# A two-layer decoder on one core: wide rope operations, two norms and a scaling moved, the constants in two transfers, two turns ahead of a bound

## The reference, cut to what matters

```python
x = x + L0_attn(layernorm(x))            # 32 heads, 8 kv heads, rope, a window mask, sinks
x = x + L0_xattn(layernorm(x), mask, ctx)
x = x + L0_ffn(layernorm(x))             # 8 experts, two for each token
x = x + L1_attn(layernorm(x))            # 16 heads of 128, 4 kv heads, rope, causal
x = x + L1_xattn(layernorm(x), ctx, m)   # "readout": softmax(x ctx^T / sqrt(512)) ctx
x = x + L1_ffn(layernorm(x))             # sigmoid * (cos + sin of tanh), 2 rounds of product and norm
# L1_attn:
q = q * cos + rotate_half(q) * sin       # k in the same way
scores = q k^T / sqrt(128);  causal mask;  softmax;  out = attn v;  out @ Wo.T
```

## Time and profile before

| | |
|---|---|
| time, median of 3 | 1766.33 us (1766.12 to 1766.53) |
| the profiled execution | 1767.63 us, its span 1765.8 us |
| busy: PE, DVE, ACT, POOL | 1705.7 (97%), 991.3 (56%), 548.0 (31%), 458.6 (26%) us |
| TensorE's granted clock, mean | 0.991 of full speed |
| the chain that ended last | PE 84%, DVE 9%, POOL 3% |

### The profile page before, as it was taken

How to read it: one execution, slowest core, us unless ns; L and a number is a source line. 1 busy time by engine, 2 the same in 40 slices (tenths; PEclk the granted TensorE clock), 3 DMA queues, 4 the chain that set the end, 5 groups by cost and what they waited for, 6 DMA issues and landing times.

```text
span 1765.8 us, 32976 instructions
## 1 busy us (share of the span) xinstructions
PE 1705.7 (97%) x13868; PEld 1141.1 (65%) x13868; DVE 991.3 (56%) x1965; ACT 548.0 (31%) x1515; POOL 458.6 (26%) x549
## 2 busy tenths in 40 slices
PE   7999999999999999999999999998999999999998
PEld 6776666657666666666546888866677774444444
DVE  3765556537767777677742111125554555664987
ACT  0343334424444444444401111101422222333411
POOL 2532322512322222222022000015131210002676
PEclk9999999999999999999989999999999999999999
DMA  9100012000000000000338988855000033752101
GB/s 400 45 1 1 1 45 70 1 27 20 19 1 19 20 1 19 19 2 1 120 140 333 344 335 330 337 196 192 1 1 1 1 137 118 245 193 84 29 13 42
DMA packets 31844, 172.48 MB, mean 98 GB/s; under 512 B 4008, under 2 KB 4008, under 8 KB 17904
## 3 DMA queue, kind: packets, MB, share of 16 engines
q1 hardware_dynamic: 29456, 163.02, 24.7%
q0 software_dynamic: 2240, 7.34, 1.2%
HBM read 155.67 MB, written 16.52 MB: 98 GB/s over the span
## 4 chain that ended last, share of the span: by engine, by line
PE 84%; DVE 9%; POOL 3%; issue 1%; ACT 1%; DMA 1%; another core or an unknown queue 0%; DVEq 0%; POOLq 0%; SPq 0%; ACTq 0%
PE PS L1308 9%; PE PS L1076 7%; PE PS L1127 6%; PE PS L1486 5%; PE PS L1377 5%; PE PS L1165 5%; PE PS L1317 4%; PE PS L1422 4%; PE PS L1455 3%; PE PS L1188 3%; PE PS L1205 3%; PE PS L1473 3%; PE PS L1135 3%; PE PS L1152 2%; PE PS L1157 2%; DVE R L1606 2%
## 5 line engine op out<-in xcount | busy, mean ns | idle before, releaser
L1308 PEld LDWEIGHTS PS<-R,W 128*128 128x128 f32 x1344 | 153.2, 192 | 11.7 <-issue 11.7
L1308 PE MATMUL PS<-R,W 128*128 128x128 f32 x1344 | 153.6, 275 | 2.2 <-DVE R L1799 2.2
L1622 DVE TENSOR_REDUCE nmw<-PS 112x2 f32<-112x750 f32 x128 | 114.1, 934 | 42.5 <-PE PS L1188 42.5
L2239 POOL TENSOR_TENSOR rstd<-veps,mhalf 128x1 f32<-128x1 f32 (+1 forms) x71 | 53.9, 759 | 322.1 <-DVE veps L1516 298.7
L1076 PE MATMUL PS<-xT,W 128*128 128x224 f32 x640 | 127.2, 358 | 1.0 <-ACT xT L2029 0.7
L1076 PEld LDWEIGHTS PS<-xT,W 128*128 128x128 f32 x640 | 121.8, 193 | 9.8 <-issue 7.6
L1806 DVE TENSOR_TENSOR R<-R,PS 128x512 f32<-128x512 f32 x21 | 14.4, 686 | 199.1 <-PE PS L1308 199.1
L1455 PE MATMUL PS<-W 128*128 128x512 f32 x256 | 119.3, 609 | 0.9 <-ACT R L2097 0.9
L2097 ACT ACTIVATE R<-PS 125x672 f32<-125x672 f32 x128 | 86.6, 730 | 86.2 <-PE PS L1205 86.2
L2265 POOL TENSOR_TENSOR R<-R 128x224 f32<-128x224 f32 x80 | 52.8, 660 | 218.6 <-DVE R L1538 218.5
L1377 PE MATMUL PS<-xT,W 128*128 128x224 f32 x512 | 103.2, 362 | 2.5 <-DVE R L1541 2.3
(11 more groups left out here) (309 smaller groups left out, 3343.5 us busy)
## 6 DMA issues: line engine op xcount, KB each, us to landing
W<-in_we SPq DMA_DIRECT2D x63, 1024.0 KB, 7.6
R<-in_ctxT SPq DMA_DIRECT2D x12, 750.0 KB, 7.1
W<-in_entwT SPq DMA_DIRECT2D x8, 1024.0 KB, 7.0
W<-in_entpw SPq DMA_DIRECT2D x8, 1024.0 KB, 8.6
R<-in_ctx SPq DMA_DIRECT2D x8, 750.0 KB
xs_rows<-in_x SPq DMA_DIRECT2D x3, 1792.0 KB, 36.1
R<-xs_rows SPq DMA_DIRECT2D x21, 256.0 KB, 8.2
ys_rows<-R SPq DMA_DIRECT2D x21, 256.0 KB, 8.2
```

The lines of the kernel that those rows point to most:

```text
L1308: o = e.matmul(PS[:, m, c * 128:(c + 1) * 128], gate_up(j % 3, k, off + c * 128), BT[:, j % 2, k, :], start=k == 0, stop=k == 3)
L1622: e.tensor_reduce(nmw[0:S, par, :].rearrange("p (r f) -> p r f", r=4)[:, r:r + 2, 16 - 16 * par], PS[0:S, r:r + 2, 0:SC], AX.X, ALU.max, n ...
```

## The change

1. **Rope.** For `kq1` (32 steps) DVE does two `tensor_tensor` operations of 448 columns instead of four of 224: one on A and B by the tables cos, sin, one by sin, cos. A second copy of the cosine table, `l1cos_`, stands behind `l1sin` for it. `ku` keeps its four.
2. **Norms of tiles 4 and 5, stage 3**: ahead of round `attend1(1)` instead of ahead of the mask of round 2.
3. **Last unit (u = 3)**: the norm of tile 0 for the readout goes behind the softmax piece `c1` of the first round, that of tile 1 behind the one of the second round, `turn` of tile 0 into the fourth. In all four rounds `d1` stands ahead of the second `v1`, so ahead of its copy on DVE.
4. **Constants**: the first transfer has the columns up to `k0sin` (576 of 2107). The rest goes ahead of `w0o`. The table `spread`, which nothing reads, is gone.
5. **Last stage**: `turnh` 0 and `turnh` 1 stand ahead of the last `bound`.

```diff
@@ constants()
+    CST["later"] = (sum(q.shape[1] for q in parts), 0)
...
     add("l1sin", np.sin(ang))
+    add("l1cos_", np.cos(ang))
...
-    add("spread", spread)
@@ build_order()
-            nxt = norms(3, bs) + nxt[:5] + turns(3, bs) + nxt[5:]
+            nxt = norms(3, bs) * (u > 0) + nxt[:5] + turns(3, bs) + nxt[5:]
...
-            nxt = norms(4, (0, 1)) + turns(4, (0,)) + [("load", "xb", 0)]
+            for n, more in enumerate((norms(4, (0,)), norms(4, (1,)), [], turns(4, (0,)) + [("load", "xb", 0)])):
+                step = attend1(4 * u + n)
+                k = step.index(("c1", u, n, 1)) + 1
+                step.insert(step.index(("v1", u, n - 1, 1) if n else ("v1", u - 1, 3, 1)), step.pop())
+                out += step[:k] + more + step[k:]
+            break
...
-            out += once[4:10] + second + once[10:]
+            out += norms(3, (4, 5)) + once[4:10] + second + once[10:]
...
-    out += [("wave", 3)] + [("bound", t) for t in range(4, NT)]
+    out += [("wave", 3)] + [("bound", t) for t in range(4, NT - 1)]
...
-    out.append(("turnh", 0, *steps[0]))
+    out += [("turnh", n, *steps[n]) for n in range(2)] + [("bound", NT - 1)]
...
-        if n + 1 < len(steps):
+        if 1 < n + 1 < len(steps):
@@ rope_in()
+                if k == "kq1":
+                    both = PS[:, m, 0:2 * UT].rearrange("p (a b n) -> p a b n", a=2, b=UB)
+                    for n, name in enumerate(("l1cos", "l1sin")):
+                        f = CST[name][0]
+                        e.tensor_tensor(T4[:, 2 * n:2 * n + 2, :].rearrange("p a (b n) -> p a b n", b=UB), both,
+                                        cst[:, f:f + 2 * S].rearrange("p (a n) -> p a n", a=2).unsqueeze(2).to_broadcast(
+                                            [128, 2, UB, S]), ALU.mult).then_inc(*up(("rope_half", "rope_in")[n], (k, u, c)))
+                    return
@@ load()
-                    put("d_cst", 0, (cst[:, :], a["consts"]), (col[:, :], a["cols"]))
+                    n = CST["later"][0]
+                    put("d_cst", 0, (cst[:, 0:n], a["consts"][:, 0:n]), (col[:, :], a["cols"]))
...
-                    put("d_w0o", 0, (W[:, 6:10, :], a["w0o"]))
+                    n = CST["later"][0]
+                    put("d_w0o", 0, (cst[:, n:NCST], a["consts"][:, n:NCST]), (W[:, 6:10, :], a["w0o"]))
```

More of the change, by code:

```diff
@@ L133, in constants @@
     add("l1sin", np.sin(ang))
+    add("l1cos_", np.cos(ang))
     add("parity", p[:, None] // 16 % 2 == np.arange(2)[None, :])
-    spread = np.zeros((128, 512), f)
-    spread[:64] = np.arange(512)[None, :] // 16 == np.arange(64)[:, None] % 32
-    add("spread", spread)
     k = np.arange(S)
```

## The result

The changed kernel takes 1756.12 us (median of 5 runs; the kernel before took 1766.33 beside it). The ratio is 0.9939, with a 95% interval of 0.9925 to 0.9953. One of its five runs took 4410.87 us and is not in the ratio. The forecast was 1757.0, the range 1754.0 to 1760.6; by the interval the gain is 8.3 to 13.2 us, so the 0.9 us between forecast and measurement can't be told from none. The profiled execution has a span of 1754.5 us (before 1765.8).

What follows compares the result with a forecast made beforehand. PE, busy in 97% of the span, was taken as the bound, with its waits and the lower clock behind them. The terms summed to 9.35 us; against the median of 1766.33 that gave 1757.0 us, range 1754.0 to 1760.6.

Steps and rivals of the forecast that it cites:

- First transfer: At the start: a shorter first transfer of constants lets the first transposes begin earlier, 0.15 us (bounds 0 and 0.5).
- Wide rope: Projection of unit 0: four ropes ahead of PE's last wait, each 0.13 us shorter, 0.5 us; hidden in units 1 to 3.
- The clock in the projection: Unit 0's projection: a quarter of a chance that the lower clock lasts 3.4 us, not 6.8, saving 1.7; term 0.4 us.
- Norms of tiles 4 and 5: Near 1260: PE's 2.48 us wait and 1.7 of clock go, less 0.4 for `ku`'s copy; 3.8 us.
- First round: Unit 3, first round: with the readout's norms behind the softmax piece, PE's wait of 1.54 us goes; term 1.5 us.
- fourth round: Unit 3, fourth round: earlier `d1` gains 1.0 us, leaves a 0.9 wait, and 1.7 of clock goes; 2.7 us.
- The last stage: Turns ahead of the last bound: copy gives 1.0, with the clock 2.7, but `waved` 6 leaves 0.3 us.
- The clock rivals: New waits, as in unit 3's fourth round or last stage, still drop the clock: 1758.7 or 1760.4 us; chance 0.22.

Runs made afterwards that it cites:

- experiment 3: Only the wide rope for `kq1`, with the table in place of the unused one, on the kernel before; ratio 0.9986.
- Experiment 8: The changed kernel with the last wave (6) one step earlier, ahead of DVE's and POOL's part of product 1; 1754.63 us, ratio 0.9933.
- experiment 1: Only the norms of tiles 4 and 5 moved ahead of round 1, on the kernel before; ratio 0.998.
- experiment 4: Only the two turns put ahead of the last bound, on the kernel before; ratio 0.9989.
- experiment 2: Only the edit of unit 3 (two norms behind softmax pieces, scaling ahead of the copy of the values), on the kernel before; ratio 0.9985.
- experiment 10: The changed kernel with the experts' rows of tiles 4, 5 and 6 added later on DVE; 1755.77 us, ratio 0.9943.
- experiment 11: The changed kernel run once more, nothing altered; 1756.94 us, ratio to the kernel before 0.9942.
- experiment 5: The kernel before with 16 products of 512 columns that nobody reads, in front of five steps where PE waits; 1764.12 us, ratio 0.9993.
- experiment 6: The kernel before with fewer such unread products in the five waits (1, 2, 2, 2, 2); 1764.09 us, ratio 0.999.
- experiment 7: The changed kernel with six unread products of 512 columns at PE's very start; 1754.49 us, ratio 0.9933.

## Why the prediction was right, and where it wasn't

- **First transfer.** Its 0.21 for 0.15 is not shown to be the edit's. In the seven traces with one transfer PE's first transposes start at 7.18 to 7.58 us (mean 7.41), in the four with two transfers at 7.26 to 7.42 (mean 7.33), so the spread is larger than the term. What came behind it, -0.65, is mostly the clock's rise, 1.06 us later in this execution than in that of before (15.85 for 14.79). In the eleven traces without fillers at the start the rise came at 13.1 to 16.0 us, for kernels with the same start too, and PE's lead at 31.5 us follows it, at some 0.5 us for each us.
- **Wide rope.** The price was right: a pair takes 1.14 us from its start to its end, as forecast. It was worth 0.41 (experiment 3), forecast 0.5. By the rule of the Trainium skill (VectorE: DVE Perf Modes, "The DRAIN you can't avoid"), taken without its exception, the term would have been 1.2; the trace disagrees, as the next operation starts 0.53 us behind one that lasts 0.61. The same section adds that an operation that is not held starts earlier, and with that the trace agrees. The step that failed is the one ahead of it, that the waits in the trace of before are the kernel's: 1.03 us of them came from a stall of DVE, probably of that execution alone (experiment 3).
- **The clock in the projection.** "A quarter of a chance of 1.7", 0.4, was mis-sized: it gave 1.26. The 6.8 us were the exception. In eight other traces with a wait of 2.2 to 2.3 us there, the stretch was 3.4 us seven times and missing once.
- **Norms of tiles 4 and 5.** Right: 3.90 for 3.8, with a new wait of 0.36 for `ku`'s copy (0.4).
- **Unit 3.** First round 1.68 for 1.5; fourth round 2.59 for 2.7, with a wait of 0.99 left (0.9). But 1.7 of the fourth round's term is a fall that this wait doesn't always cause.
- **The last stage.** Right: the copy gives 1.04 (forecast 1.0), and `waved` 6 takes back what the clock and the copy give, but for 0.51 (0.3). Experiment 8 shows the cause of the wait that is left.
- **The clock rivals.** The reading of the earlier trace rows, that 1.54 us keep the clock and 1.86 lose it, was too simple. Behind 1.86 us at 1475 the clock fell in 2 of 4 traces (before and experiment 1, not 3 and 4), behind 1.94 at 1650 in 2 of 4 (before and experiment 1 again, not 2 and 3), behind 2.48 at 1260 in 4 of 4. Waits of 1.10 to 1.25 us, which every trace has near 1310, were followed by a fall in 3 of 14, one of 1.5 us near 1447 in none of 6. By the eight cases with 1.9 us (five traces) such a wait costs itself and some 0.85, an estimate. The prediction also passed over layer 0, where much shorter waits were followed by a fall. Windows of the kernel before:

```profile
885.20:892.00 6.80, 5.94 (x49) 2.81 (x44) 0.28 (x1) 1.35 (x2) 0.00 (x0) 0.50 0.02 4
909.10:912.50 3.40, 3.40 (x6) 1.48 (x6) 2.74 (x13) 0.00 (x0) 0.00 (x0) 0.50 0.99 419
```

  Ahead of the first stand waits of 0.73 and 0.82 us, ahead of the second one of 0.78. All 14 traces fall near 886 and 13 near 909, and in the two traces of the table they are equally long, so they left the sum alone, but they speak against any limit near 1.8 us. When the clock rose at the start seems to matter: in the four traces with a rise at 13.1 to 13.4 us (experiments 1, 8, 10, 11) it fell near 747, behind a wait of 0.96, each time; in the seven with a rise at 14.8 to 16.0 never; of the three with fillers at the start (5.0, 5.8, 6.3) in the first two. The Trainium skill (TensorE: Matmul & The Clock Gate, Part 1) says that the clock's watch runs free of the kernel, so that one kernel starts up differently from run to run; the start agrees (13.08 and 15.85 us for the same kernel). That it holds for falls in the middle too would fit these counts, but no run tests it.

So the total came out near the forecast partly since errors of both signs met: 1.65 us too little in the projection, 0.65 too much at the start. The medians are 10.2 us less in the result and 9.5 in experiment 11, not 11.2. There a part of the falls is missing on the side of before: its 69 timed executions have a median granted clock of 0.993 where the profiled one has 0.991. The nine executions of the changed kernel that the two ratios rest on have 0.995, so by an estimate (0.002 of 1764 us) some 3.5 us of the gain are the clock's. That the stall is missing as well is argued, not measured.

What stays open: the cause of DVE's stall, and what decides whether a given wait is followed by the lower clock in one execution and not in the next.

## What to carry to other kernels

Price a wait of the engine that sets the end from the trace, but price the clock behind it from several executions: here one profile held a stall of 1.0 us, and falls that other traces with the same waits lacked (two of them behind waits of 1.9 us). Before a wait is removed, read what the same stage waits for next (wave 6), and ask whether that one only stands in the wrong place of a queue; moving it was worth more than twice what the turns were. A wait that can't be removed can be filled with work that nobody reads, if the filler's length is measured first; here such fillers kept the clock up, but no run shows a gain in time from them that is clear of the noise.

## What the runs showed of the hardware

- An fp32 product of 512 columns is two matmuls in the trace and took 0.86 us from start to start at the upper level (3.44 for four).
- Products in a wait keep the granted clock at 1.00 behind it: so at all eight filled places of experiments 5 and 6, where without fillers it fell in 8 of 9 traces (1220, waits of 2.2 to 2.3 us), 4 of 4 (1260), 2 of 4 (1475) and 2 of 4 (1650). The mean granted clock was 0.996 or more in 12 of 12 and 8 of 12 executions of these two kernels, and in 4 of 69 of the kernel before.
- The clock can fall behind waits of PE of under 1 us (0.73 and 0.82 us near 884, in 14 of 14 traces) and stay up behind 1.94 (2 of 4): the length of one wait doesn't decide it.
- PE starts at about half pace, and the profile's clock column doesn't show it; work from 1.45 us on brought the first record to 4.97, 5.84 and 6.29 us in three traces; without it, it came at 13.1 to 16.0 in eleven.
- Outside the clock, executions mostly agree: five waits in two executions of one kernel differed by no more than 0.02 us. A sixth differed by 0.10 us, and was some 0.3 us shorter in experiments 7 and 8, whose edits lie elsewhere.
